# Numbering a mixture-of-experts' slots in three levels, sending rows in parts of 16, 8 and 8 tiles, and leaving out PE's blank matmuls in one step of attention's drain

## The reference

```
x = layernorm(x + attention(x))        # 16 heads of 8, softmax over 256 keys, head mask
x = layernorm(x + moe(x))
moe(x) = shared(x) + sum over the token's 2 best of 8 experts of gate * expert(x)
shared, expert = gelu_tanh(x @ Wfc + bfc) @ Wproj + bproj      # 128 -> 512 -> 128
gate = softmax(x @ Wr), the best two, divided by their sum
```

## Time and profile before

| | us |
|---|---|
| median of 3 executions (lowest, highest) | 517.65 (517.15, 518.68) |
| the profiled execution's own time | 515.57 |
| its span in the profile | 513.8 |
| busy: PE, DVE, ACT, POOL | 418.1, 361.1, 329.2, 322.4 |

### The profile page before, as it was taken

One profiled execution on the slowest core, in us unless ns is written; L12 is line 12 of the kernel. 1 busy time (PEld: TensorE's weight loads), 2 busy tenths in 40 slices (PEclk: granted clock), 3 DMA queues, 4 the chain that ended last, 5 costly groups with the idle time before them and its releaser, 6 DMA issues. The chain is left out here.

```text
span 513.8 us, 13680 instructions
## 1 busy us (share of the span) xinstructions
PE 418.1 (81%) x4871; PEld 277.4 (54%) x4871; DVE 361.1 (70%) x765; ACT 329.2 (64%) x624; POOL 322.4 (63%) x427
## 2 busy tenths in 40 slices
PE   4999999999999999999965888604999999999000
PEld 2444454555545555545542665503999999998000
DVE  3567888787888788788681698502778777777582
ACT  1147888788878888878714997302666776676162
POOL 4402678566573758565356666666688778877651
PEclk9999999999999999999986999956999999999655
DMA  3322554635454455521101111145371111117142
GB/s 87 89 59 65 157 158 115 177 102 145 115 159 122 138 142 157 166 76 34 42 17 46 43 49 43 48 113 156 101 210 42 49 44 48 43 31 264 50 147 61
DMA packets 63110, 50.25 MB, mean 98 GB/s; under 512 B 7339, under 2 KB 54581, under 8 KB 63045
## 3 DMA queue, kind: packets, MB, share of 16 engines
q1 hardware_dynamic: 58500, 40.91, 28.0%
q0 software_dynamic: 4544, 8.47, 5.2%
HBM read 24.96 MB, written 22.95 MB: 93 GB/s over the span
## 5 line engine op out<-in xcount | busy, mean ns | idle before, releaser
L553 DVE TENSOR_REDUCE row_max<-s_ps 128x2 f32<-128x512 f32 x256 | 164.9, 683 | 45.7 <-PE s_ps L684 43.7
L413 ACT ACTIVATE probs<-ring_ps 128x1024 f32<-128x1024 f32 x128 | 130.7, 1022 | 46.3 <-PE ring_ps L702 45.9
L1496 POOL DMA_INDIRECT results<-gated,rows_in x78 | 91.9, 1178 | 26.5 <-issue 22.6
L1652 ACT ACTIVATE hid<-h_ps,bias 128x256 f32<-128x256 f32 x156 | 61.1, 474 | 64.3 <-PE h_ps L1586 64.3
L684 PE MATMUL s_ps<-qk_stack 24*128 24x256 f16 x512 | 83.5, 271 | 7.1 <-DVE row_max L553 2.6
L1337 POOL DMA_INDIRECT slots<-rows,slot_at x64 | 65.8, 1028 | 29.4 <-issue 17.2
L702 PE MATMUL ring_ps<-qk_stack 26*128 26x256 f16 x512 | 83.0, 271 | 0.0
L720 PE MATMUL av_ps<-probs,v_aug 128*32 128x256 f32 x1024 | 68.5, 385 | 0.0
L684 PEld LDWEIGHTS s_ps<-qk_stack 24*128 24x128 f16 x512 | 33.8, 92 | 61.5 <-issue 32.4
L1604 PE MATMUL y_ps<-w,hid 128*128 x312 | 57.7, 220 | 0.0
L1605 PE MATMUL y_ps<-w,hid 128*128 x312 | 57.5, 219 | 0.0
(11 more groups left out here) (218 smaller groups left out, 953.6 us busy)
## 6 DMA issues: line engine op xcount, KB each, us to landing
qk_stack<-qk_rows SPq DMA_DIRECT2D x64, 96.0 KB
slots<-empty_row SPq DMA_DIRECT2D x13, 390.0 KB, 5.0
qk_rows<-qk_parts SPq DMA_DIRECT2D x16, 256.0 KB, 2.6
rows<-results SPq DMA_DIRECT2D x8, 512.0 KB, 6.5
rows_in<-slots SPq DMA_DIRECT2D x2, 1300.0 KB, 9.5
w_stage<-in_w_fc SPq DMA_DIRECT2D x9, 256.0 KB, 3.2
w_stage<-in_w_proj SPq DMA_DIRECT2D x9, 256.0 KB, 3.7
rows_in<-slots SPq DMA_DIRECT2D x1, 2080.0 KB, 10.2
```

The costliest lines, as they stand in the source:

```text
L413: nc.scalar.activation(probs[:, n % PROBS], ring(key), ACT.Exp, scale=SCORE_SCALE).then_inc(ring_emptied, 1)
L553: nc.vector.tensor_reduce(row_max[:, h], s1_ps[:, h % 2], AX_X, ALU.max, negate=True).then_inc(max_done, 1)
L1496: nc.gpsimd.indirect_dma_start(out=a["results"][:, :], out_offset=bass.IndirectOffsetOnAxis(ap=rows_in[:, 2 * n + half, DEST:DEST + 1].bit ...
L1652: mm = nc.scalar.activation(hid[:, cols], h_ps[:, cols], ACT.Gelu_apprx_tanh, scale=1.0 / UNIT, bias=bias[:, n, c:c + 1])
```

## The change

**Numbering.** `SHARES` becomes `PASSES = ((0, 24), (24, 32))` for the routing and `SENT = ((0, 16), (16, 24), (24, 32))` for the sends. The first pass numbers its slots in three levels: the blocks that are full after 16 tiles (at least 9), those that are full after 24 (at least 17 in all), and those that are still partly filled; the second pass adds its blocks behind them. So 32 sends (tiles 0 to 15, both choices) complete the first 9 blocks, 48 the first 17. **Loads.** SP loads slot tiles 0 to 1 and 2 to 17 after 32 sends, 18 to 33 after 48, and 34 to 77 in three parts after all 64. **Order in steps 17 and 18.** The second `pick` moves ahead of batch 13's residual; the counts move from PE's pair 5 to pair 3 and on ACT from behind pair 5's exponentials to behind pair 3's, with the exponential of the gap ahead of them; `gate` and the first `place` move from step 18 to step 17. POOL sends 2 tiles at the start of step 18 and 4 at its end. **Blank matmuls.** The three `keep_clock(4)` of step 17 are left out, those of steps 18 and 19 stay. **Second pass.** `claim`, `offset` and `jump` become `extend`, `add_blocks` and `jump_last`; the table of experts is made in two parts, the second one (`finish_table`) four units later than the first.

```diff
 MAX_UNIT = 256.0
-SHARES = ((0, 24), (24, 32))
+PASSES = ((0, 24), (24, 32))
+SENT = ((0, 16), (16, 24), (24, 32))
 ROUTE_STEP = 17
 TURNED_EARLY = 7
-PLACED = {18: (0, 4)}
+PLACED = {18: (2, 4)}
 WEIGHT_ORDER = (8, 0, 1, 2, 3, 4, 5, 6, 7)
 CAST_AT = (4, 5, 7, 9, 11, 12, 13, 14, 15)
...
 PROBS = 6
-Q_AT, K_AT, TURN_AT, LOGIT_AT, COUNT_AT = 0, 3, 2, 6, 5
+Q_AT, K_AT, TURN_AT, LOGIT_AT, COUNT_AT = 0, 3, 2, 6, 3
 
 
 
...
                     evacuate("k", ahead, bk)
+                if t == ROUTE_STEP:
+                    share_gap(nc, act, a, 0)
+                    take_counts(0)
                 if late.exists():
                     exp_pair(late, 4)
                 if t == 2:
@@ -510,9 +514,6 @@
                     exp_pair(late, 5)
                 if now.exists():
                     evacuate_max(now, 0)
-                if t == ROUTE_STEP:
-                    take_counts(0)
-                    share_gap(nc, act, a, 0)
                 if late.exists():
                     exp_pair(late, 6)
                 if last.exists():
...
                     router.pick(0, 0)
+                    router.pick(0, 1)
                 if now.exists():
                     largest(now, 0)
                     largest(now, 1)
@@ -616,11 +618,8 @@
                 if now.exists():
                     for h in range(4, 8):
                         largest(now, h)
-                if t == ROUTE_STEP:
-                    router.pick(0, 1)
                 if t == ROUTE_STEP + 1:
-                    router.gate(0)
-                    router.place(0, 0)
+                    router.place(0, 1)
                 if last.exists():
                     invert_sums(last)
                     normalise(last)
@@ -628,16 +627,16 @@
                     for h in range(8, HEADS):
                         largest(now, h)
                 if t == ROUTE_STEP:
+                    router.gate(0)
                     counts_taken(0)
                     router.tally(0)
-                    router.fill_whole()
-                    router.begin_parts()
-                    router.claim(0)
-                    router.offset(0)
-                    router.rank(0)
+                    router.level()
+                    router.lay_out()
+                    router.order(0)
+                    router.jump_levels()
+                    router.place(0, 0)
                 if t == ROUTE_STEP + 1:
-                    router.place(0, 1)
-                    router.move_on(0)
+                    router.carry()
 
...
                     if p == 0:
-                        if not now.exists():
+                        if not now.exists() and t != ROUTE_STEP:
                             keep_clock(4)
                         if gone.exists():
...
                             project("k", ahead, wk)
-                        if not now.exists() and last.exists():
+                        if not now.exists() and last.exists() and t != ROUTE_STEP:
                             keep_clock(4)
                         if last.exists():
...
                                 pe.wait_ge(max_evacuated, 2 * now.n + 1)
-                            if not now.exists():
+                            if not now.exists() and t != ROUTE_STEP:
                                 keep_clock(4)
                             turn_heads(last)
...
-                    first, rest = FIRST_TILES // EMPTY_TILES, -(-SLOT_TILES // EMPTY_TILES)
-                    pool.wait_ge(a["slots_emptied"][c], 16 * (first, rest - first)[c])
+                routed = [c for c, (first, end) in enumerate(PASSES) if first <= lo < end][0]
+                pool.wait_ge(a["slots_known"], TOP * routed + k + 1)
+                if n == 0:
+                    pool.wait_ge(a["slots_emptied"], 16 * -(-SLOT_TILES // EMPTY_TILES))
                 if k == 1:
                     pool.wait_ge(a["rows_copied"][c], 16 * (hi - lo) // GROUP)
             nc.gpsimd.indirect_dma_start(out=a["slots"][:, :], out_offset=bass.IndirectOffsetOnAxis(
                 ap=a["slot_at"][:, k, tile:tile + 1], axis=0), in_=a[("rows1", "rows2")[k]][:, tile], in_offset=None)\
-              .then_inc(a["rows_placed"][int(c > 0)], 16)
+              .then_inc(a["rows_placed"][c], 16)
             if (n + 1) % PAUSE_EVERY == 0:
-                pool.wait_ge(a["rows_placed"][int(c > 0)], 16 * (n + 1 - TOP * lo))
+                pool.wait_ge(a["rows_placed"][c], 16 * (n + 1 - TOP * lo))
 
 
...
-        FIRST, FULL, LOAD = 2, 2 * FULL_BLOCKS, 20
+        LOADS = (0, 2, 2 * FULL_BLOCKS[0], 2 * FULL_BLOCKS[1], 44, 60, SLOT_TILES)
...
             copy_rows(sp, a, LAST_GROUP)
-            sp.wait_ge(a["rows_placed"][0], 16 * TOP * SHARES[0][1])
-            load_slots(0, FIRST, first_loaded)
-            load_slots(FIRST, FULL, full_loaded)
-            sp.wait_ge(a["rows_placed"][1], 16 * TOP * (TOKEN_TILES - SHARES[0][1]))
+            sp.wait_ge(a["rows_placed"][0], 16 * TOP * (SENT[0][1] - SENT[0][0]))
+            load_slots(0)
+            load_slots(1)
+            sp.wait_ge(a["rows_placed"][1], 16 * TOP * (SENT[1][1] - SENT[1][0]))
+            load_slots(2)
+            sp.wait_ge(a["rows_placed"][2], 16 * TOP * (SENT[2][1] - SENT[2][0]))
             sp.wait_ge(table_made, 1)
-            for lo in range(FULL, SLOT_TILES, LOAD):
-                load_slots(lo, min(lo + LOAD, SLOT_TILES), rest_loaded)
+            for k in range(3, len(LOADS) - 1):
+                load_slots(k)
             for buf in range(RING):
                 sp.wait_ge(sent[buf], 32 * times_sent(buf, EARLY_BLOCKS))
             for g in range(EARLY_GROUPS):
...
-                if n == 0:
-                    pe.wait_ge(first_loaded, 16)
-                if n == FIRST // 2:
-                    pe.wait_ge(full_loaded, 16)
-                if n == FULL_BLOCKS:
-                    pe.wait_ge(rest_loaded, 16 * -(-(SLOT_TILES - FULL) // LOAD))
+                if 2 * n in LOADS:
+                    pe.wait_ge(slots_in[LOADS.index(2 * n)], 16)
                 if n >= 2:
                     pe.wait_ge(slots_taken, n - 1)
```

More of the change, by code:

```diff
@@ L954, in make_moe_buffers @@
     a["slot_at"] = sb("slot_at", [P, TOP, TOKEN_TILES], U32)
[L955 to L958 removed]
+    for name, rows in (("reached", LEVELS + 1), ("passing", LEVELS + 1), ("fills", LEVELS), ("begins", LEVELS), ("moved", LEVELS),
+                       ("jumps", LEVELS - 1)):
+        a[name] = sb(name, [P, rows, EXPERTS])
+    most = max(hi - lo for lo, hi in PASSES)
     a["rest"] = sb("rest", [P, most, EXPERTS])
@@ L968, in make_moe_buffers @@
     a["full"] = sb("full", [P, EXPERTS, MOST_BLOCKS])
[L969 to L970 removed]
+    for name in ("taken", "base", "more", "fresh", "starts", "last_jump"):
         a[name] = sb(name, [P, EXPERTS])
```

204 lines of the change are left out of this document (73 added, 131 removed).

## The result

The changed kernel takes **522.06 us** (median of 8 executions, 518.79 to 524.00), the kernel before beside it 517.40 (8, 516.10 to 519.75): ratio 1.0072, 95% interval 1.0041 to 1.0104. So 4.7 us were lost where 1.8 were forecast as won, outside the range. The profiled execution took 523.27 us with a span of 521.5, 7.7 more than in the profile before.

What follows compares the result with a forecast made beforehand. The prediction took POOL's list of sends to bound the kernel: -0.3 (start) + 2.2 (placing) - 3.7 (results) + 0 (tail) = -1.8 us, so 515.8 us, 0.35% less, with a range of 512.5 to 520.

Steps and rivals of the forecast that it cites:

- Which engine ends last: Whole kernel: POOL's list of indirect DMAs from 261.64 to 484.0, plus a 29.8 us tail, sets the end, not PE.
- the ring: Second stage: weigh(8) needs block 0's results landed, so PE stands 9 us near 366 to 375, using up its former gap.
- the gap does come back: Rival, faster: PE is the bound and its first blocks come 19 us earlier, 498.7 us; chance 0.07.
- Where POOL starts: Steps 17 and 18: slot numbers at 261.5 (260.8 to 263), seventh send at 278.7 instead of 279.0, so -0.3 us.
- the 0.3 allowed for the clock: Step 17: PE's lower clock adds about 0.7 us to slot numbers at 261.2, giving 261.9; 261.5 was taken.
- POOL's halves beside DVE's chain: Steps 17 and 18: halve counted only within POOL's unchanged 14.7 us; no slowing of DVE's numbering was priced.
- The blank matmuls: Step 17: three sets of 0.9 us each are covered by DVE's and ACT's waits, so leaving them out gains nothing.
- The placing: Placing sends beside 10 early blocks: 4.2 us added less 2.0 already paid, +2.2 us (bounds 0 and +9.1).
- The results: Results' 78 sends: 111.7 instead of 115.4 us, since fewer blocks' splits lie beside them; -3.7 us (bounds 0 and -5).
- The tail: From POOL's last send to the end: hangs on that send as now, 29.8 us, change 0.
- The sends collide more: Rival, slower: placing sends blocked for all of L1745 and L1738, +5.1 us, 522.8; chance 0.22 (0.20 slower).
- the cancelling rival: Rival, same: the results gain just what the placing loses, leaving -0.3 us, 517.4 us; chance 0.13.

Runs made afterwards that it cites:

- l1: g1's kernel with only the high-by-high one of PE's three products of halves in the second stage; 518.98 us, ratio 1.0026 to the kernel before.
- g1: The changed kernel with the second pick back behind batch 13's residual; 518.18 us against 517.42 for the kernel before, ratio 1.0020.
- e2: The kernel before without the three sets of blank matmuls of step 17; ratio 1.0130 in a series where PE has gaps.
- e1: The changed kernel with the three sets of blank matmuls of step 17 back; ratio 1.0084 in a series where PE has gaps.
- e4: The changed kernel with SP's first two loads only after 48 sends; ratio 1.0090 in a series where PE has gaps.
- l2: l1's kernel with SP's first two loads only after 48 sends; 520.43 us, ratio 1.0059 to the kernel before.
- h3: The kernel before with SP's wait for the 48 sends written nine times; ratio 1.0116 in a series where PE has gaps.
- h2: The kernel before with PAUSE_EVERY = 16, four of eight placing pauses gone; 571.96 us against 551.71, in a series where PE has gaps.
- f2: g1's kernel with SP's first two loads only after 48 sends; ratio 1.0201 in a series where PE has gaps.
- h1: g1's kernel with SP's first two loads only after 48 sends; 553.41 us against 551.71, where PE has gaps.
- k1: g1's kernel with SP's first two loads only after 48 sends; 552.13 us against 550.12, where PE has gaps.
- f4: The kernel before with 16 more semaphores, each raised by a small memset on DVE; ratio 1.0043 in a series where PE has gaps.

## Why the prediction was wrong

- **Which engine ends last: right.** POOL's waits in the results are 73 times 0.3 us of issue, PE's gap went to the ring (ACT waits 8.6 us there, PE 5.0 where 9 were forecast), a third of PE's products changed nothing (l1), and 3.5 us off the seventh send took 2.7 to 3.9 off the time (g1). The rival "the gap does come back" is out.
- **Where POOL starts: the step that failed.** The text put the slot numbers at 261.5, 18.7 us from the first pick, and the seventh send at 278.7; they came at 20.7 and at 38.7 in place of 35.9. The 2.0 us of the numbers are, by the forecast's own points: ACT's copy of the maxima 0.5 later (6.4 us, not 5.9); from there to the counts' copy 0.4 more (4.0 for 3.6), at the lower clock; `gate` not half but wholly behind it, 0.8 more (1.2 for 0.4), because the sums of the heads ahead of it came late from PE and its COPY took 0.66 us; the numbering 9.2 us for 8.5, one instruction of `level` taking 1.03 us in place of 0.26; less the 0.3 allowed for the clock. The 0.8 behind them are the wait for batch 14 and the small sums named above. The text had seen that the late exponentials "take back what the earlier counts were to give" and stopped there. It never worked out the same list with the pick left late: that gives counts at 6.1 us and numbers at 17.6 (g1), 3.1 us earlier.
- **POOL's halves beside DVE's chain: a term put at nothing.** The two long instructions add 0.47 and 0.77 us, 1.2 of the 2.0. In every profile of the changed kernel and its variants one to three of DVE's small instructions in `gate` or the numbering are stretched in this way, the COPY of `gate` to 1.16 us in g1 (252.30 to 253.46, POOL's L1073 252.25 to 253.41), and each begins behind the start of POOL's instruction and ends 0.04 to 0.42 us behind its end. In the kernel before the halves (L1072 and L1074, 250.79 to 252.66) lay in DVE's wait for the counts and cost this path nothing. That DVE is held by POOL's instruction is read from these times; no run moves the halves away to prove it. The late pick does not avoid it.
- **The blank matmuls: wrong in the old order.** "Leaving them out gives nothing on this path": e2 gains 1.3 us, and e1 loses 0.8 or more by having them back. The second set stands between the turn of the maxima and the counts, on the path and not behind the waits. The clock did fall as the text feared, but for 17 us, and the text priced it in three groups of matmuls only, 0.7, of which it took 0.3. Between e4 and the changed kernel, where it fell 2 us apart, lie 0.9 us; what a clock that never falls would give in this order, no run shows.
- **The placing: mis-sized, +3.0 for +2.2.** The mean of all 64 sends rose from 1.028 to 1.059 us, 2.0 in all, as each block's splits stretch a send; 0.9 more are in the pauses, of which two end at 313.05 and 338.53 after 2.38 and 3.25 us instead of 1.6. No load of SP lies beside them (its first two run from 325.25 to about 331), and the trace shows no reason; g1 has one of 2.27, l2 one of 2.70.
- **The results: mis-sized, -2.5 for -3.7.** The mean of 78 sends fell from 1.177 to 1.145 us.
- **The tail: 0 forecast, +1.3.** It did hang on POOL's last send, but the end behind the last write is longer, for a reason not found.
- **The rivals.** "The sends collide more" has the right sign by another cause: its 5.1 us rested on a placing 9.1 us longer, and that took 3.0. With the second pick late (g1) the outcome is near the cancelling rival: +0.8 us by the medians (0 to 2.2 by the interval) where that had -0.3. In g1's profile placing, results and tail add to nothing (+1.4, -2.8, +1.4) and the seventh send is 1.0 us earlier, so medians and single profiles differ here by about 2 us.

None of the kernels tried beats the kernel before where that could be told. e2, with the seventh send 1.3 us earlier, was run only where PE has gaps, and was not faster there (1.0130, 1.0085 to 1.0174).

## What to carry to other kernels

When a chain of small instructions is moved ahead of an engine's other work, follow not the chain but what it now stands in front of: here 3.1 us of pick in front of one residual delayed the counts that the pick was for. Price filler matmuls on the path by the instruction behind them, not by the mean idle time of the engines around them. Look at what the other engines do at the place where a chain moves to: here DVE's numbering came to lie beside POOL's halves and was 1.2 us longer for it. And with single profiles align at a point that the change cannot have moved: two executions of the same attention code differed by 2.9 us there.

## What the runs showed of the hardware that I had not expected

- The same program runs in two regimes. In six of eight series the kernel before took 545 to 562 us instead of 517, with its first pick as early as ever (243.5 to 244.7), and gaps of 0.5 to 1.9 us between PE's matmuls of the second stage in which PE waited for nothing shown. Sends of POOL that come more densely go with larger gaps: PE's listed waits of that kind from 285 to 345 sum to 16 us with a pause each eighth send (h3) and to 31 with one each sixteenth (h2), and the time rises by 5%. So these pauses may protect PE; that is an inference from three runs of one edit, not a mechanism shown.
- The granted clock fell to 0.50 behind a wait of PE of 3.4 us and stayed there for about 17 us though PE was busy throughout (254 to 268 above). Such a wait does not decide it alone: with PE's list and its wait of 1.8 us for `chosen` alike, it fell in g1 and f2 and not in h1 and k1; and behind the same wait of 0.80 us it fell in f4 and not in the kernel before.
- A DVE instruction of 0.14 to 0.56 us that starts beside an arithmetic instruction of POOL on SBUF can last until POOL's has ended, up to 1 us more (in all twenty profiles one to three such places; in the kernel before 0.89 us for 0.36 at 264.36, beside POOL's 264.31 to 265.03).
- The end of the program behind the last write is one of two lengths, 1.3 us apart, by kernel and not by execution.
